# First attention of a two-layer graph network: a ring of eight probability slots, and Gelu, residual sums and norm statistics moved in between its blocks

## The reference

```python
# x: 3327 x 256 (padded to 26 tiles of 128 rows), adj: 3327 x 3327
def gnn(X, A, W, r):                      # X = layernorm(x)
    Wh = X @ W.T
    e = (Wh @ r_src)[:, None] + (Wh @ r_dst)[None, :]
    e = where(e >= 0, e, 0.2 * e)
    e = where(A == 0, -inf, e)
    return gelu(softmax(e, axis=1) @ Wh)
x = x + gnn(layernorm(x), adj, ...)
xn = layernorm(x)
x = x + experts(xn)                       # router: softmax(xn @ gate_w + gate_b), top 2 of 8 experts
```

## Time and profile before

| | |
|---|---|
| median of 3 runs | 2019.82 us (2018.22 to 2021.35) |
| profiled execution | 2017.3 us, span in the trace 2015.4 us |
| TensorE busy | 1665.5 us, 83% of the span |
| VectorE busy | 980.1 us, 49% |
| ScalarE busy | 1033.3 us, 51% |
| matmuls of the first attention (L884), 128x257 | 277.1 us and 24.0 us |
| stage of the first attention | from about 135 to 472 us |

### The profile page before, as it was taken

One profiled execution on the slowest core, in us unless ns is written; L12 is line 12 of the kernel. 1 busy time (PEld: TensorE's weight loads), 2 busy tenths in 40 slices (PEclk: granted clock), 3 DMA queues, 4 the chain that ended last, 5 costly groups with the idle time before them and its releaser, 6 DMA issues. The chain is left out here.

```text
span 2015.4 us, 43515 instructions
## 1 busy us (share of the span) xinstructions
PE 1665.5 (83%) x12926; PEld 1536.0 (76%) x12927; DVE 980.1 (49%) x2116; ACT 1033.3 (51%) x2127; POOL 497.2 (25%) x558
## 2 busy tenths in 40 slices
PE   4649999994589997473897997979965899999998
PEld 3538888883579997353896897879965799999997
DVE  4638788885712222665765766756666111111111
ACT  1634444443245554114886787877843354545453
POOL 1100000000056765007605307200000233333332
PEclk9969999995689999696998999999975899999999
DMA  9960000003367776400000000000044566666664
GB/s 148 108 129 8 16 8 8 21 0 110 110 186 203 204 203 149 156 13 6 11 8 17 16 4 23 10 14 14 11 152 152 186 182 178 180 181 181 180 182 108
DMA packets 81365, 190.04 MB, mean 94 GB/s; under 512 B 9562, under 2 KB 52854, under 8 KB 72470
## 3 DMA queue, kind: packets, MB, share of 16 engines
q1 hardware_dynamic: 48438, 138.73, 21.0%
q0 software_dynamic: 27280, 45.56, 14.2%
q10 hardware_dynamic: 5584, 4.99, 0.8%
HBM read 189.37 MB, written 33.11 MB: 110 GB/s over the span
## 5 line engine op out<-in xcount | busy, mean ns | idle before, releaser
L1213 PE MATMUL bank<-arena 128*128 128x195 bf16 x5408 | 479.0, 249 | 104.8 <-DVE arena L1114 44.3
L1213 PEld LDWEIGHTS bank<-arena 128*128 128x128 fp8e4 x5408 | 467.6, 98 | 116.2 <-issue 114.6
L1024 ACT ACTIVATE arena<-arena,m_row 128x512 fp8e5<-128x512 f32 (+1 forms) x728 | 431.8, 677 | 132.8 <-DVE arena L1114 120.5
L1667 PEld LDWEIGHTS bank<-X,arena 128*128 128x128 f32 x2832 | 337.8, 194 | 6.5 <-DMA arena<-m0w 0.5
L1667 PE MATMUL bank<-X,arena 128*128 128x128 f32 x2832 | 338.2, 277 | 0.1
L1705 PE MATMUL bank<-arena,X 128*128 x1416 | 329.2, 383 | 4.6 <-ACT X L1740 4.4
L1764 DVE TENSOR_TENSOR arena<-bank,X 128x256 f32<-128x256 f32 x118 | 50.1, 425 | 559.0 <-PE bank L1705 552.3
L884 PE MATMUL bank<-arena 128*128 (+1 forms) x1352 | 299.6, 383 | 15.5 <-DVE arena L827 15.5
L884 PEld LDWEIGHTS bank<-arena 128*128 128x128 f32 x1352 | 257.1, 191 | 57.2 <-issue 21.4
L1705 PEld LDWEIGHTS bank<-arena,X 128*128 128x128 f32 x1416 | 260.8, 191 | 42.0 <-issue 11.0
L805 ACT ACTIVATE bank<-arena,s_all 128x384 f32<-128x384 f32 (+1 forms) x234 | 134.0, 573 | 183.8 <-DVE arena L819 175.8
(11 more groups left out here) (208 smaller groups left out, 1434.5 us busy)
## 6 DMA issues: line engine op xcount, KB each, us to landing
arena<-m1w SPq DMA_DIRECT2D x67, 1024.0 KB, 12.0
arena<-m0w SPq DMA_DIRECT2D x67, 512.0 KB, 8.0
arena<-adjT POOLq DMA_DIRECT2D x26, 416.0 KB, 12.8
xs<-X SPq DMA_DIRECT2D x4, 1664.0 KB, 6.9
arena<-qd SPq DMA_DIRECT2D x25, 256.0 KB, 3.2
xe<-zeros POOLq DMA_DIRECT2D x1, 3456.0 KB, 14.5
X<-x_in SPq DMA_DIRECT2D x2, 1664.0 KB, 11.2
xd<-X SPq DMA_DIRECT2D x13, 256.0 KB, 2.1
```

The lines of the kernel that those rows point to most:

```text
L1024: last = a.activation(self.sign[slot].bitcast(F8W)[:, q * W:q * W + nt * P], self.row[r][:, 0:nt * P], ACT.Sigmoid, scale=STEEP, bias=self ...
L1213: last = pe.matmul(bank[r * NT + n][:, kind * KW:(kind + 1) * KW], self.split[slot][kind].bitcast(F8)[:, q * W + n * P:q * W + (n + 1) * P ...
L1667: last = pe.matmul(bank[2 * s + c // 4][:, c % 4 * P:(c % 4 + 1) * P], self.W1[s][:, k * HID + c * P:k * HID + (c + 1) * P], self.rxt[s][: ...
```

## The change

The ring gets eight slots (`RING = 8`), and the loops over chunks go in groups of eight; 26 chunks are three groups and two. VectorE's and ScalarE's blocks are written out one by one instead of in a loop over pairs of blocks.

ScalarE's Gelu comes in parts: pairs of tiles 0 to 3 between blocks 3 and 4, pairs 4 to 8 between blocks 6 and 7, pairs 9 to 11 behind the last block's Exps, and pair 12 after the last `normalise`. After each of the first two parts an Exp on one column of ones (`exp_again`) is added.

VectorE adds pairs 0 to 3 in block 5 and pairs 4 to 6 in block 7, each after the eighth chunk; it takes the statistics of pairs 0 to 3 in block 6 and of pairs 4 to 6 in block 8, at the same place. Behind block 8 come pairs 7 and 8, pairs 9 to 11, and only then the last `normalise` and pair 12. The router of the first layer takes no statistics any more (`done=True`); that of the second still does.

```diff
-                self.slots = 2 if H > 1 else 4
+                self.slots = 2 if H > 1 else self.RING
...
             def each_chunk(self, eng, body):
-                with eng.Fori(0, T // 4) as i:
-                    for q in range(4):
-                        body(4 * i + q, q, i)
-                for q in range(T % 4):
-                    body(T // 4 * 4 + q, q, T // 4)
+                R = self.RING
+                with eng.Fori(0, T // R) as i:
+                    for q in range(R):
+                        body(R * i + q, q, i)
+                for q in range(T % R):
+                    body(T // R * R + q, q, T // R)
...
+            def gelu_pairs(self, a, first, last):
+                for i in range(first, last):
+                    o = self.attn_out[:, i * 2 * D:(i + 1) * 2 * D]
+                    a.activation(o, o, ACT.Gelu).then_inc(self.out_ready, 1)
...
+                def exp_again():
+                    a.activation(self.exp_spare, ones_t[:, 0:1], ACT.Exp)
+
+                for b in range(4):
+                    block_of(b, self.nt)
+                a.wait_ge(self.banks_free[0], 3)
+                self.gelu_pairs(a, 0, 4)
+                exp_again()
+                for b in range(4, 7):
+                    block_of(b, self.nt)
+                a.wait_ge(self.banks_free[1], 4)
+                self.gelu_pairs(a, 4, 9)
+                exp_again()
+                block_of(7, self.nt)
+                block_of(8, self.L.tail // P)
+                a.wait_ge(self.banks_free[1], 5)
+                self.gelu_pairs(a, 9, 12)
+                a.wait_ge(self.banks_free[0], 6)
+                self.gelu_pairs(a, 12, PAIRS)
...
+                def add_pairs(first, last):
+                    for i in range(first, last):
+                        v.wait_ge(self.out_ready, i + 1)
+                        xs_ = X[:, i * 2 * D:(i + 1) * 2 * D]
+                        v.tensor_tensor(xs_, xs_, self.attn_out[:, i * 2 * D:(i + 1) * 2 * D], ALU.add
+                                        ).then_inc(self.x_added, 1)
+
+                def stats_of(first, last):
+                    for i in range(first, last):
+                        v.wait_ge(self.x_added, i + 1)
+                        for t in (2 * i, 2 * i + 1):
+                            v.bn_stats(stats[:, t * 6:t * 6 + 6], X[:, t * D:(t + 1) * D]).then_inc(stat, 1)
+
+                def block_of(b, nt):
+                    larger(b, nt, 0, 0, 0)
+                    for q in range(R):
+                        larger(b, nt, q + 1, (q + 1) % R, (q + 1) // R)
                         masked(b, nt, q, q, 0)
+                        if q == 3 and b > 0:
+                            normalise(b - 1, nt_)
+                    if b == 5:
+                        add_pairs(0, 4)
+                    if b == 6:
+                        stats_of(0, 4)
+                    if b == 7:
+                        add_pairs(4, 7)
+                    if b == 8:
+                        stats_of(4, 7)
...
+                for b in range(L.blocks):
+                    block_of(b, nt_)
+                block_of(L.blocks, L.tail // P)
+                add_pairs(7, 9)
+                stats_of(7, 9)
+                add_pairs(9, 12)
+                stats_of(9, 12)
+                normalise(L.blocks, L.tail // P)
+                add_pairs(12, PAIRS)
+                stats_of(12, PAIRS)
...
-                layer_norm_stats(v, self)
+                layer_norm_stats(v, self, done=not self.second_norm)
```

More of the change, by code:

```diff
@@ L274, in __init__ @@
                     k += T * D
+                    self.exp_spare = words(k, 1)
+                    k += 1
                 assert k <= ARENA, (tag, k)
@@ new lines, in stats_of, with block_of @@
+                def stats_of(first, last):
[3 more added lines that the diff above has]
+                            v.bn_stats(stats[:, t * 6:t * 6 + 6], X[:, t * D:(t + 1) * D]).then_inc(stat, 1)
+                def block_of(b, nt):
+                    larger(b, nt, 0, 0, 0)
+                    for q in range(R):
+                        larger(b, nt, q + 1, (q + 1) % R, (q + 1) // R)
+                        masked(b, nt, q, q, 0)
+                        if q == 3 and b > 0:
[8 more added lines that the diff above has]
+                        stats_of(4, 7)
+                    n = T // R
+                    with v.Fori(1, n) as i:
+                        for q in range(R):
+                            larger(b, nt, R * i + q + 1, (q + 1) % R, i + (q + 1) // R)
+                            masked(b, nt, R * i + q, q, i)
+                    larger(b, nt, T - 1, 1, n)
+                    for q in range(2):
+                        masked(b, nt, R * n + q, q, n)
+                    v.wait_ge(self.prob_ready[1], (b + 1) * self.ring_uses(1))
+                    v.sem_inc(self.rows_free[b % 2], 1)
@@ L891, in single_tensor @@
                 self.each_block(pe, body)
-            def gelu_scalar(self, a):
-                a.wait_ge(self.banks_free[0], self.L.blocks // 2 + 1 + 1)
-                for i in range(PAIRS):
-                    o = self.attn_out[:, i * 2 * D:(i + 1) * 2 * D]
-                    a.activation(o, o, ACT.Gelu).then_inc(self.out_ready, 1)
-            def gelu_vector(self, v):
-                with v.Fori(0, PAIRS) as i:
-                    v.wait_ge(self.out_ready, i + 1)
-                    xs = X[:, at(i * 2 * D, 2 * D)]
-                    v.tensor_tensor(xs, xs, self.attn_out[:, at(i * 2 * D, 2 * D)], ALU.add
-                                    ).then_inc(self.x_added, 1)
             def gelu_sync(self, sp):
```

49 lines of the change are left out of this document (18 added, 31 removed).

## The result

The changed kernel took 2000.63 us (median of 4 runs, 2000.59 to 2003.20), the kernel before in the same comparison 2020.07 us (2018.22 to 2021.35): ratio 0.9906, 95% interval 0.989 to 0.9921. Forecast was 2008.6, with a range of 2003.5 to 2014.0: the kernel is faster, as forecast, and by more than the range held. The profiled execution took 2000.6 us, its span 1998.6.

The account below looks back on a forecast made before the run. TensorE was taken to set the pace inside the first attention, with 29.4 us without a matmul behind it. Tail -3.2 and router -8.0 gave -11.2: 2006.1 for the profiled execution, 2008.6 for the median, range 2003.5 to 2014.

Parts of the forecast that it names:

- Eight slots by themselves: First attention's ring: costed at nothing; seams stay 0.92 per block, and VectorE gains a lead of 5 to 6 chunks.
- the 6 x 0.18: TensorE's short waits after a block's fourth chunk, during VectorE's normalise; eight slots were said not to help there.
- The batches are hidden: Gelu batches on ScalarE behind blocks 3 and 6 cost nothing, with slack of 2.7 and 1.1 us.
- The rival's price for four slots: Rival that batches do not fit: with four slots' lead they stick out 2.7 in all; 2010 to 2013, chance 0.14.
- VectorE's own pace: VectorE in the attention blocks, unblocked: 0.99 us a chunk, plus 0.24 at a loop head.
- the price of the insertions: Sums and statistics after chunk 7 in blocks 5 to 8: TensorE waits 1.4, 1.6, 0.8, 1.65, 5.5 later in all.
- the loop head of 0.24: VectorE's pause at a loop head, counted between each insertion and chunk 8 in blocks 5 to 8.
- The tail: Attention's end: last normalise 8.7 later, but 11.9 of store issues gone, so the stage ends 3.2 earlier.
- The router: Router stage loses 8.69 of statistics, 0.7 returns as TensorE's wait for the second router load: net 8.0 saved.
- Behind it everything shifts: Stages behind the router's start only move earlier, and the router loop runs as before with TensorE's clock fallen to 1.2 GHz.
- The last 2.5: Whole kernel: profiled execution 2.5 under the runs' median, so 2006.1 forecast for a like execution and 2008.6 for the median.
- the three signs that I named for a wrong forecast: First attention: a seam with a batch opens, VectorE's in-loop pitch exceeds 1.1, or the last normalise finds VectorE idle.

Follow-up runs that it names:

- e1: Kernel before with only the eight slots and written-out blocks, Gelu, sums and statistics as before: 2019.63 us against 2018.87, ratio 1.0004.
- e15: Repeat of e1, eight slots and written-out blocks alone on the kernel before: 2020.91 us against 2018.92, ratio 1.0013.
- e2: Changed kernel with four slots instead of eight, all else kept: 2003.48 us against 2018.87 for the kernel before, ratio 0.9922.
- e6: Changed kernel with sums and statistics put in after chunk 15 instead of 7, chunk-group loop written out: 1997.86 us against before's 2016.64, ratio 0.9905.
- e10: Eight slots, all Gelus at the end, each pair's statistics in the tail, none in the router: 2014.57 us against before's 2018.19, ratio 0.998.

## Why the prediction was off

**Eight slots by themselves, no gain and no loss: right in the main.** The seams stayed. But I had left the 6 x 0.18 in the sum as waits that stay, and the written-out blocks don't have that pause (0.20 inside `normalise`). Worth 0.9 at TensorE's end (from block 1 to its last matmul 273.63 before, 272.70 in e1 and 272.69 in e15). What the slots do buy, 1.9 at the last reciprocal, was in the sum unseen, since the tail was worked out with VectorE's full lead.

**The batches are hidden: right.** Slack 3.7 and 2.0 behind two Exps, forecast 2.7 and 1.1 behind one; a second Exp takes some 0.5, so the slack was 1.4 to 1.5 larger than forecast. VectorE waited 7.42 at the seam instead of some 6. The next ACTIVATE began 0.02 behind the table load's end (275.25 + 1.28 to 276.55), and 0.01 at the way back. The Trainium skill (ScalarE: Activation LUTs, What ACT_TABLE_LOAD costs) adds 1.38 of drain to a switch; no switch of this case shows it. The rival's price for four slots failed: e2 shows 0.2 where I had 2.7. It left out the 0.7 by which `larger` 0 may be late, though the prediction says that `larger` 1 waits for the later chunk. The first batch made it only 0.4 late (a wait of 2.79 instead of 2.37).

**VectorE's own pace: the step that failed, and with it the price of the insertions.** The term was 1.4 + 1.6 + 0.8 + 1.65 = 5.5 later at TensorE. Counted from block 1, TensorE's last matmul came 3.6 later than before's (277.22 against 273.63). The insertions cost 4.5 of delay (against the 272.70 of e1, which has none); the pauses gave 0.9 back. Each of the four is too dear by the same amount, the loop head of 0.24 that I added behind the insertion. VectorE goes from its last sum to the next `larger` with no gap:

```profile
331.35 2.49 DVE L882 TENSOR_TENSOR X<-X,arena 128x512 f32<-128x512 f32 x4
333.76 0.61 DVE L854 SCALAR_TENSOR_TENSOR arena<-arena,d_all,bank 128x384 f32<-128x384 f32 x1
```

In block time chunk 8 started at 11.86 in block 5, where I had 12.3: 0.24 of that is the head, 0.16 the pause. The heads are gone in every other place as well, with e1's edit alone; why, no run tells. e6 shows that nearly all of the 4.5 could be hidden too.

**The tail: mechanism right, size off by what stands before it.** Counted from block 1, VectorE's last `masked` ended at 273.3 where I had 276.1 (456.5 - 180.37): six heads of 0.24 that were not there, 1.4; the pauses, 0.9; and the last two `masked`, which end 0.34 apart and not 0.73, 0.4. From the last `masked` to the last reciprocal I had 6.4, and it took 6.4 (453.97 to 460.41). From there to the next stage it took 5.4 (460.41 to 465.78) where I had 6.0 (3.06 + 2.9). Together the stage ended 6.3 earlier instead of 3.2.

**The router: right.** 7.5 instead of 8.0, with the wait for `gate_b` that was forecast. TensorE's clock was granted in full until about 462, 4 us behind its last matmul, and the router ran at 0.50. Before's clock fell in the same way, and its router's window from 488 to 500 has 0.50 too. Windows of the changed kernel:

```profile
461.00:462.00 1.00, 0.00 (x0) 0.00 (x0) 0.54 (x2) 0.43 (x1) 0.00 (x0) 0.95 0.25 84
462.00:463.00 1.00, 0.00 (x0) 0.00 (x0) 0.73 (x2) 0.20 (x1) 0.00 (x0) 0.50 0.00 0
...
480.00:490.00 10.00, 10.00 (x54) 10.00 (x53) 3.56 (x9) 6.55 (x17) 0.00 (x0) 0.50 0.00 0
```

**"Behind it everything shifts", and the scatter.** The forecast for the median was 8.0 too high (2008.6 against 2000.63). 2.7 of it arose up to the router (13.9 earlier instead of 11.2), and that is the part that is shown: heads 1.4, pauses 0.9, the last `masked` 0.4 and the tail's 0.6, less the 0.5 that the router gave less than forecast, 2.8 of the path. It is no scatter, since the path is 14.0 shorter in the mean of three profiles. Another 2.9 came behind the router in the first profile. The last 2.5 is the distance that I put between the profiled execution and the median, because before had it; in the first comparison the changed kernel's profiled execution took 2000.60 and its median is 2000.63.

These last two were the luck of a draw to a good part. From the router's first matmul to the end, the changed kernel's three profiles take 1528.8, 1534.5 and 1532.0, in the mean what before's two take (1531.8 and 1531.9). Its later medians, 2003.99 and 2002.53, lie on either side of the range's lower end. Over 16 runs the gain is 16.7, which is 2.7 more than the path, give or take some 1.2; five profiles don't show where that lies, and it stays open. The rhythm of the experts' tiles is one part of the scatter between programs that was found, and it works against e1 and e10, not for the changed kernel, whose tiles take as long as before's. Eight slots alone lose 1.7 and 4.1 behind their shorter path (totals of +0.5 and +2.8 with 1.3 less of it), and a delay of 3.5 cost -1.0. The second layer's stages, too, differ between profiles of one kernel: its attention, from the start of ScalarE's first table load to that of its last activation (line L1069), takes 570.6, 572.5 and 572.6 in the three of the changed kernel. So the second step that failed is to hold the stages behind the router rigid. The range of 5 us below the forecast had room for scatter or for the mis-sized terms, but not for both.

None of the three signs that I named for a wrong forecast came: no seam opened at a batch, VectorE's pitch inside the loop was 0.99, and the last `normalise` did not find it idle. All three looked for a kernel slower than forecast, and the miss was on the fast side.

## What to carry to other kernels

Before pricing a deeper ring, find where its lead is used. At the seams a second instruction waited a chunk longer, and four slots did nearly as well as eight; at the end of the last block the lead of eight slots let the producer's tail begin 1.9 us sooner. Work put on a busy engine belongs where its lead is largest and behind the last link of the path, not in front of it: the same instructions moved eight chunks later, and six of them behind the last `normalise`, made the path 5.1 us shorter still. To compare edits of a few us, measure between two events that both lie behind the first scattering stage: from block 1 the path repeated to 0.2 us, while its end counted from the start of the span moved by 0.9 in one kernel. Later stages with the same instructions are not rigid, so a range has to hold their scatter.

## What the runs showed of the hardware that was not expected

ScalarE's time to issue the same instruction in the same loop was 0.7 us in fourteen profiles and 0.9 in six, by the program, and the stage takes 5.4 more in the six (262.6 against 257.2 in the mean). TensorE's clock in the second layer's values stage rose sooner in the changed kernel: its first transpose there is at 820.45 and the window to 826 has a mean of 0.61, whereas before it is at 834.62 and the window to 840 has 0.50. Windows of the changed kernel, then of before:

```profile
816.00:826.00 10.00, 7.27 (x28) 6.13 (x29) 5.69 (x24) 1.31 (x4) 0.00 (x0) 0.61 0.00 0
```

```profile
830.00:840.00 10.00, 7.15 (x23) 5.66 (x24) 4.91 (x21) 0.97 (x3) 0.00 (x0) 0.50 0.01 2
```

From that transpose to ScalarE's first table load of the attention it took 71.3 us in the one and 73.3 in the other, but 73.1 and 72.5 in the changed kernel's other two profiles, so it is no property of the change.
